# A decoder layer in split fp32 on one core: context rows at another spacing, operands at one remainder of 512 bytes, one attention sum moved behind its step's projections

## The reference

```python
x = layernorm(x + self_attention(x))        # relu(q k^T) * R_hat(|i - j|), causal, softmax, @ v, @ Wo + bo
x = layernorm(x + cross_attention(x, ctx))  # q from x; k and v from ctx (32, 722, 512); softmax; @ Wo.T + bo
x = layernorm(x + ffn(x))                   # (silu(x Wg) * (x Wu)) Wd, hidden 1536, integer weights / 127
```

## Time and profile before

| | |
|---|---|
| median of 3 runs | 2403.01 us (2401.48 to 2404.96) |
| the profiled execution | 2403.05 us, its span 2401.2 us |
| TensorE busy | 98% of the span |
| VectorE, ScalarE, GpSimd | 63%, 55%, 58% |
| granted TensorE clock | 0.995 of 2.4 GHz |

### The profile page before, as it was taken

How to read it: one execution, slowest core, us unless ns; L and a number is a source line. 1 busy time by engine, 2 the same in 40 slices (tenths; PEclk the granted TensorE clock), 3 DMA queues, 4 the chain that set the end, 5 groups by cost and what they waited for, 6 DMA issues and landing times.

```text
span 2401.2 us, 58639 instructions
## 1 busy us (share of the span) xinstructions
PE 2346.0 (98%) x21642; PEld 2039.1 (85%) x21642; DVE 1511.3 (63%) x2563; ACT 1331.8 (55%) x3322; POOL 1384.2 (58%) x1211
## 2 busy tenths in 40 slices
PE   8999979999999999999999999999999899999999
PEld 7888858988888888888888888888888699998998
DVE  4666688837666666667666666667676734435342
ACT  5878862136666666666666666666666651221321
POOL 4767577357657667566666667666665533333332
PEclk9999999999999999999999999999999999999999
DMA  7444468636677677777776776776677831101010
GB/s 190 132 128 106 118 194 315 226 104 189 185 198 202 192 190 199 190 205 196 187 202 191 192 205 187 194 203 192 181 199 204 245 129 42 49 17 66 5 35 23
DMA packets 254121, 384.59 MB, mean 160 GB/s; under 512 B 116056, under 2 KB 131480, under 8 KB 253848
## 3 DMA queue, kind: packets, MB, share of 16 engines
q1 hardware_dynamic: 229272, 330.65, 48.6%
q10 hardware_dynamic: 24576, 50.36, 8.2%
HBM read 126.33 MB, written 40.60 MB: 70 GB/s over the span
## 4 chain that ended last, share of the span: by engine, by line
PE 75%; DVE 1%; issue 1%; SPq 1%; DMA 1%; POOL 0%; ACT 0%; ACTq 0%; POOLq 0%; DVEq 0%
PE D_ps_p L68 42%; PE D_ps_s L1956 7%; PE E_ps_g L68 6%; PE D_ps_p L1983 6%; PE E_ps_u L68 6%; PE E_ps_d L68 5%; PE E_ps_y L68 3%; SPq L1369 1%; PE E_ps_t L2012 0%; DMA D_pT<-D_turned 0%; DVE D_columns L1753 0%; DVE D_turned L1767 0%; DMA E_x_last<-x 0%; ACT D_e L1618 0%; POOL E_x1b L1518 0%
## 5 line engine op out<-in xcount | busy, mean ns | idle before, releaser
L1481 POOL TENSOR_SCALAR D_e<-D_e,D_columns 128x722 f32<-128x722 f32 x256 | 538.9, 2105 | 468.5 <-DVE D_columns L1759 468.5
L1618 ACT ACTIVATE D_e<-D_ps_s,D_columns 128x723 f32<-128x723 f32 x512 | 438.3, 862 | 391.4 <-DVE D_columns L1753 347.6
L1753 DVE TENSOR_REDUCE D_columns<-D_ps_s 128x1 f32<-128x723 f32 x512 | 439.5, 899 | 296.3 <-PE D_ps_s L1956 296.1
L1767 DVE STREAM_TRANSPOSE D_turned<-D_e 128x768 f32<-128x768 f32 x512 | 496.2, 972 | 16.3 <-DMA D_pT<-D_turned 15.1
L68 PE MATMUL D_ps_p<-D_ctx_high,cross_wk_high 128*128 128x362 f32 (+1 forms) x1024 | 350.1, 342 | 2.3 <-DVEq L1779 1.4
L68 PE MATMUL D_ps_p<-D_ctx_low,cross_wk_high 128*128 128x362 f32 (+1 forms) x1024 | 336.6, 329 | 0.0
L68 PE MATMUL D_ps_p<-D_ctx_high,cross_wk_low 128*128 128x362 f32 (+1 forms) x1024 | 334.8, 327 | 0.0
L68 PE MATMUL D_ps_p<-cross_wv_high,D_ctx_high 128*128 128x512 f32 (+1 forms) x656 | 259.7, 396 | 0.0
L68 PE MATMUL D_ps_p<-cross_wv_high,D_ctx_low 128*128 128x512 f32 (+1 forms) x656 | 259.3, 395 | 0.0
L68 PE MATMUL D_ps_p<-cross_wv_low,D_ctx_high 128*128 128x512 f32 (+1 forms) x656 | 257.7, 393 | 0.0
L1625 ACT ACTIVATE D_e<-D_e,D_columns 128x722 f32<-128x722 f32 x256 | 230.9, 902 | 6.9 <-DVE D_columns L1759 6.9
(11 more groups left out here) (264 smaller groups left out, 5243.6 us busy)
## 6 DMA issues: line engine op xcount, KB each, us to landing
D_pT<-D_turned SPq DMA_DIRECT2D x1536, 96.0 KB
D_pT<-D_turned ACTq DMA_DIRECT2D x512, 96.0 KB
D_craw<-in_ctxT SPq DMA_DIRECT2D x124, 361.0 KB, 4.0
self_v<-wstage SPq DMA_DIRECT2D x25, 256.0 KB, 2.5
A_v<-self_v SPq DMA_DIRECT2D x32, 200.0 KB
self_o<-A_o SPq DMA_DIRECT2D x32, 200.0 KB, 3.6
x<-C_x SPq DMA_DIRECT2D x5, 1280.0 KB, 5.8
cross_q<-C_qo SPq DMA_DIRECT2D x20, 320.0 KB, 3.9
```

Of the source, the lines that this page charges most:

```text
L1481: pool.tensor_scalar(head, head, inv[:, 2 * (s % 2):2 * (s % 2) + 1], None, ALU.mult)\
L1618: act.activation(e[n // 2 % 2][:, n % 2, 0:PARTS * PART].rearrange("p (a c) -> p a c", a=PARTS), parts_of(n), ACT.Exp, bias=neg_max[:, n % ...
L1753: dve.tensor_reduce(neg_max[:, n % 4:n % 4 + 1], parts_of(n), AX.XY, ALU.max, negate=True)\
L1767: dve.transpose(turned[quad % 2][:, :, 2 * (s % 2) + h, :].rearrange("p j (t r) -> p t j r", r=32), e[s % 2][:, h, :].rearrange("p (t j r) ...
```

## The change

A chunk of a context takes 768 elements (`ROW`, 3072 bytes, six times 512) in place of 722; the last 46 are not read. The keys' halves are columns 0 to 384 and 384 to 722. `tails` moves up in SBUF, and so do `E_wo` and the weights of gate and up, so that everything which TensorE reads with them begins at remainder 288: both contexts, `tails`, `cross_wk`, `cross_wv`, `E_acts`, `E_wo`, and pieces 0 to 4 of the feed forward weights. Part A's, part C's and `E_ps_d`'s operands stay where they were.

The room for it comes from `tails_raw`, two chunks of 384 in place of four; a chunk is loaded when the one two before has been split, with three DMAs for each chunk (12 for four sequences, 6 before), at three places of SP's queue. The step at which GpSimd splits each chunk is as before. The last of the first five tiles of x1 is loaded into `E_x2` after the last unit has read its weights, two moves later in SP's queue. GpSimd waits for VectorE's last look at the integers before it writes `D_ctx0_low`, which now reaches into `C_ints`.

In part A up to step 28 the weighted sum stands in slot 3, behind the step's last unit and the scores; ScalarE takes its result a step later, and `store_o` comes a step later.

```diff
-        HALVES = ((0, 362), (362, S))
+        HALVES = ((0, ROW // 2), (ROW // 2, S))            # ROW = 768
-        cs = [ctx0, Split(inputs, "D_ctx1", [P, KD, S])]
+        cs = [ctx0, Split(inputs, "D_ctx1", [P, KD, ROW])]
-        craw = [inputs(f"D_craw{i}", [P, S]) for i in range(2)]
-        tails_raw = inputs("D_tails_raw", [P, KD, 3 * P])
         tails = Split(inputs, "D_tails", [P, KD, 3 * P])
         fourth = [inputs(f"D_values_fourth{i}", [P, D]) for i in range(2)]
+        craw = [inputs(f"D_craw{i}", [P, S]) for i in range(2)]
+        tails_raw = inputs("D_tails_raw", [P, 2, 3 * P])
...
+                pool.wait_ge(biggest_done, 3 * KD)
                 for k in range(KD):
                     pool.wait_ge(ctx0_high, k + 1)
...
-                        if i == 1 and s >= 3:
+                        if i == (1 if s > LAST_UNITS else 3) and s >= 3:
                             weighted_sum(s - 3)
...
-                        if s > LAST_UNITS + 1 and i == 1:
+                        if b > 0 and i == 1:
                             take_result(b - 1)
...
-                        if 0 <= b and s <= LAST_UNITS and i == 2:
-                            take_result(b)
...
-                    if s >= 4:
+                    if 5 <= s <= LAST_UNITS + 1:
+                        store_o(s - 5)
+                    if s > LAST_UNITS:
                         store_o(s - 4)
...
                     move(QUADS * b)
+                    if b % 4 == 1 and b // 4 < FOURS:
+                        load_tails(b // 4, 2)
                     if b > 0:
                         store(b - 1)
...
                     if b % 4 == 3 and (b + 1) // 4 < FOURS:
-                        load_tails((b + 1) // 4)
+                        load_tails((b + 1) // 4, 0)
+                        load_tails((b + 1) // 4, 1)
                     move(QUADS * b + 1)
+                    if b % 4 == 1 and b // 4 < FOURS:
+                        load_tails(b // 4, 3)
...
                 sp.wait_ge(u_done, len(unit_count))
+                load_first_x1(TT - 1)
                 load_weights(0)
```

More of the change, by code:

```diff
@@ L9 @@
 B, T, S, D, H = 32, 100, 722, 512, 16
+ROW = 768
 HD = D // H
@@ L1137, in phase_cross_and_feed_forward @@
         x1b = [middle(f"E_x1b{i}", [P, D]) for i in range(2)]
-        first_x1 = [*x1b, None, None, middle("E_x1_last", [P, D])]
-        r = {"a": middle("E_r_a", [P, D])}
+        r = {"a": even("E_r_a", [P, D])}
         y = [middle(f"E_y{i}", [P, D]) for i in range(2)]
[L1141 to L1145, removed]
+        stats = {n: middle("E_stats_" + n, [P, 6]) for n in "ab"}
+        mv = {n: middle("E_mv_" + n, [P, 2]) for n in "ab"}
+        var_eps = {n: middle("E_var_eps_" + n, [P, 1]) for n in "ab"}
+        rstd = {n: middle("E_rstd_" + n, [P, 1]) for n in "ab"}
         EARLY = 5
@@ L1151, in phase_cross_and_feed_forward @@
         x2 = first("E_x2", [P, TT, D])
+        first_x1 = [t[:, :] for t in (*x1b, *y)] + [x2[:, TT - 1, :]]
         r["b"] = odd("E_r_b", [P, D])
@@ L1325, in x1_rows @@
         def x1_rows(g, i):
-            return (x1b[i % 2] if later(g) else first_x1[i])[:, :]
+            return x1b[i % 2][:, :] if later(g) else first_x1[i]
         def place(t, n):
@@ L1343, in load_ctx, with load_tails @@
                     sp.dma_start(craw[k % 2][:, :], c_rows[b, :, k, :]).then_inc(c_loaded[k % 2], 16)
[L1345 to L1353 removed]
+                def load_tails(q, k):
+                    n = KD * q + k
+                    wait(sp, t_low, n - 1)
+                    shared = tails_raw[:, k % 2, :].rearrange("p (i c) -> p i c", c=P)
+                    sp.dma_start(shared[:, :, 0:LAST], c_rows[4 * q + 2:4 * q + 5, :, k, FULL:S].rearrange("b p t -> p b t"))\
+                      .then_inc(t_loaded[k % 2], 16)
+                    sp.dma_start(shared[:, 0:2, P - THIRD:P],
+                                 c_rows[4 * q + 5, :, k, FULL:FULL + 2 * THIRD].rearrange("p (i t) -> p i t", t=THIRD))\
+                      .then_inc(t_loaded[k % 2], 16)
+                    sp.dma_start(shared[:, 2, P - THIRD:P - THIRD + LAST - 2 * THIRD], c_rows[4 * q + 5, :, k, FULL + 2 * THIRD:S])\
+                      .then_inc(t_loaded[k % 2], 16)
                 def load_q(b):
@@ L1439, in _, with load_first_x1 @@
                 sp.dma_start(bo_b[:, :], bo.rearrange("(a n) -> a n", a=1).broadcast_to([P, D])).then_inc(bo_loaded, 16)
-                for i in range(TT):
-                    sp.dma_start(first_x1[i][:, :], x1_d[col(i * P, P), :]).then_inc(x1_loaded[i % 2], 16)
+                def load_first_x1(i):
+                    sp.dma_start(first_x1[i], x1_d[col(i * P, P), :])\
+                      .then_inc(x1_loaded[i % 2] if i < TT - 1 else x1_last_loaded, 16)
+                for i in range(TT - 1):
+                    load_first_x1(i)
                 move(last - 3)
```

43 lines of the change are left out of this document (19 added, 24 removed).

## The result

The changed kernel takes 2386.93 us (median of 6 runs, 2385.6 to 2389.27), the kernel before 2403.11 (6 runs, 2401.07 to 2406.29): a ratio of 0.9933, 95% interval 0.992 to 0.9945. That is 16.2 us less, where 26 were forecast. The profiled execution took 2386.26 us.

What follows compares the result with a forecast made beforehand. TensorE, busy 98% of the span, was taken as the bound, with part D's units 42% of the chain. Gains of 8.2 + 4.5 + 1.1 + 11.9 = 25.7 us off 2403.0 gave 2377 us; range for 8 in 10: 2364 to 2393.

Steps and rivals of the forecast that it cites:

- Part D is a plain sum of spacings: Part D: TensorE hardly waits, so each nanosecond off a matmul's start to start is a nanosecond off the kernel.
- With one remainder a stream settles at 13.3 ns over its columns: TensorE's streams: operands sharing one remainder of 512 settle there after some matmuls; with mixed remainders they never settle.
- The rival that the remainder sets nothing: Part D: the remainder does not set the spacing, only part A's gain is left, 2391 us; chance 0.14.
- the one of steps of 32 columns: Part D: 338 columns fit in 11 steps of 13.33 ns and values settle for good, 2362 us; chance 0.09.
- The rival of the bad phase: Part D: one remainder on both sides is the bad phase, values and keys get slower, 2409 us; chance 0.06.
- Values units, 8.2 us: Part D: 2220 values matmuls go from 232.2 to 228.5 ns, saving 8.2 us; ends 2.7 and 12.2.
- Keys units, 4.5 us: Part D: a pair of keys matmuls goes from 330.5 to 327.4 ns over 1536 pairs, 4.8 us, taken as 4.5.
- E_ps_y, 1.1 us: Part E: 300 matmuls, now at 288 on both sides, go from 232.7 to about 229 ns, saving 1.1 us.
- The weighted sums, 11.9 us: Part A: sums moved behind unit and scores save 9.0 of waits, 1.1 at step 28, 1.8 of returns; ends 6 and 14.
- 9.0 waits removed of 10.0: Part A, 60 to 300 us: of TensorE's 10.0 us waiting for the sums' blocks, 9.0 us would go.
- part A gives little: Part A: the chain behind the scores, not TensorE, sets the pace, 6 in place of 11.9, 2385 us; chance 0.12.
- The edits costed at nothing: GpSimd's wait before D_ctx0_low (else 3.5 us), the tails' twelve DMAs and the later x1 tile load: covered, no cost.

Runs made afterwards that it cites:

- the 128-byte kernel: The changed kernel with both contexts, the tails and part E's tiles in their place moved up by 128 bytes: 2402.17 us.
- another kernel with the same order in part A: The changed kernel with part A's weighted sums, their results and stores put back as in the kernel before: 2388.68 us.
- two orders: On the kernel before, part A's weighted sums moved as in the change, and VectorE's second half of the maxima put ahead of the first transposes: together 2387.7 us.
- the first edit: Part A's weighted sums moved to slot 3 up to step 28; with only this on the kernel before, 2398.34 us.
- the sums alone: The kernel before with only part A's weighted sums moved to slot 3 up to step 28, results and stores a step later: 2398.34 us.
- the two shifts: The changed kernel with contexts, tails and part E's tiles in their place moved up by 128 bytes, 2402.17 us, or by 256 bytes, 2388.38 us.
- the paired values: The changed kernel with part D's values units of even steps moved behind the next step's keys unit, so two values units follow each other: 2394.87 us.
- the halves of 362: The changed kernel with the keys' halves cut at 362 and 360 columns as before, rows of 768 kept: 2390.79 us.

## Why the prediction was right, and where it was not

The forecast was 2377 us, the time 2386.9: inside the range of 2364 to 2393, faster as forecast, but 10 us above the likeliest case. Most of these 10 us are one term, the weighted sums of part A. By its steps:

- **Part D is a plain sum of spacings.** Right. The spacings of its units give 10.6 us; the weighted sums' own spacings and the idle time take back 1.7, which leaves the 8.9.
- **With one remainder a stream settles at 13.3 ns over its columns.** Right for the widths of this kernel, and now shown by moving nothing but addresses, with two corrections: the remainder of 256 counts, and at 448, 402 and 274 columns it is 15 to 17 ns. The rival that the remainder sets nothing (2391) fell with the 128-byte kernel, and so did the one of steps of 32 columns (2362): 338 columns settle at 153 to 154 ns, between the 146.7 and the 160.0 of such steps. The rival of the bad phase (2409) has its phase, but at 128 bytes apart, not at 0. The Trainium skill, TensorE: Matmul & The Clock Gate, Back-to-back issue gap, gives N/2.4 + 2.5 ns for an isolated warm matmul, in which no address stands, 215.8 ns for 512 columns. No run here shows that: in these streams 512 columns take 226.7 ns settled and up to 236 unsettled, by address and by the stream before, and the measurement decides.
- **Values units, 8.2 us.** The mechanism right, the size off: 5.4 measured. I took 228.5 ns because "most of a run should be settled". In this kernel a values unit behind keys starts the stream anew, and of its twelve matmuls nine go by unsettled. The mean came down by 2.4 ns, not 3.7.
- **Keys units, 4.5 us.** 5.2 measured.
- **E_ps_y, 1.1 us.** From the last unit of D to the end it is 1.9. The units settle.
- **The weighted sums, 11.9 us.** This is the step that failed. The profiled pair shows 5.9, and not all of that is the sums': 3.4 us is what the kernel before lost at half clock behind two of its waits, and an execution of another kernel with the same order in part A was free of that. By the timed runs the sums are worth 3.3 us on the kernel before and 3.5 on the rest of the change (16.2 against 12.7). The starts of part D say the same when all executions are taken: 494.4 us on average with the old order (two of them), 491.5 with the new one (six). What failed was "9.0 waits removed of 10.0". The waits were removed, 9.6 of 10.0, but I looked only at what the sum waits for and at what is queued behind its new place, not at what TensorE would reach sooner. That was its PSUM buffers, which ScalarE empties behind exponentials, which wait for maxima, which stood behind transposes. The rival "part A gives little" had the time (2385) and the right kind of cause, a chain behind the scores; it blamed GpSimd, and the runs put it on VectorE's order. Its time came near for a second reason that is luck: it took 13.8 us for parts D and E, which gave 10.8.
- **The edits costed at nothing.** They cost nothing that shows. GpSimd began D_ctx0_low at 477.21, right behind VectorE's last look, took 6.29 us and had 6.60 left until part D's first work. No sum of part D waits for a move, so the twelve DMAs of the tails stayed under cover.

Still open: why a shared remainder settles a stream at all, why values settle at once behind 448 columns, after four spacings behind 274 and after nine behind 384, why 448, 402 and 274 columns stay at 15 to 17 ns over, and which of TensorE's waits of about 2 us are followed by half clock.

## What to carry to other kernels

Before a wait is priced as gain, ask which buffer or queue the freed engine reaches next, and who empties it: here two orders, each worth 3 to 4 us alone, were worth 14 together, and the trace of the first edit named the second. Where long streams of matmuls bound a kernel, put the moving operand and the weights at one remainder of 256 bytes, and measure each width that you use. A new order that keeps one width longer has 30 or 40 ns a unit to win at most; here it lost more than that in the first spacings of the second units and in one wait. And look at the granted clock beside every wait of TensorE: the wait may cost as much again.

## What the runs showed of the hardware

- The distance of a matmul's two operands modulo 256 bytes changes its spacing in a stream. At 0, 512 columns settle at 226.7 ns, 384 at 173.3 and 338 at 153.4, all 13 ns over their columns, but 448 run at 203, 402 at 185 and 274 at 129 to 130, 15 to 17 over; at 128, part D, otherwise the same, is 16 us longer (1385.6 for 1369.7).
- How many matmuls the settled state takes depends on the width that went before: 512 columns had it from the first spacing behind 448, after four behind 274 and after nine behind 384. Behind a unit of the same width it is kept only sometimes: 11 of 57 second units had it from their second spacing.
- Six executions with the very same orders in part A (the changed kernel, the sums alone, the two shifts, the paired values, the halves of 362) began part D between 490.20 and 493.95 us. A single pair of profiles can't price an edit of part A to better than some 4 us.
- After 2.0 us without work TensorE ran at 0.50 of its clock for 3.4 us, 1.7 us lost; after 2.4 us, elsewhere in the same trace, it did not.
